# Statistics of a graph layer's later groups, four weight units and the first gathered tile at other places of a one-core kernel

## The chip, the cores and the metric

The kernel runs on one core of a Trainium2 chip. What counts is the device time of one execution in microseconds (us); three executions of the kernel before took 749.41 to 750.44 us, their median is 750.01 us.

## The reference

1250 nodes with 512 features, 40000 edges. A layer norm gives `xn`; a graph layer (own features and the mean over the neighbours, each through a 512x512 matrix, then a layer norm and a relu) and a linear attention over 8 heads are both taken from `xn` and added to `x`. Then follows a feed-forward part with a shared branch and eight experts, of which every node uses two:

```python
xn = _layernorm(x)
x = x + gnn(xn, edges) + mix(xn)
flat = _layernorm(x) * ln_scale + ln_bias
h_shared = swiglu(flat @ shared_in_w.T)              # 2 x 1024 columns
out_shared = h_shared @ shared_out_w.T + shared_out_b
...                                                  # group by argmax, two experts by top_k
h_expert = swiglu(flat @ expert_in_w.T)
for e in range(8):
    routed = routed + comb[:, e:e + 1] * (h_expert @ expert_out_weight[e].T)
return x + out_shared + routed
```

## The kernel before

The nodes lie in ten tiles of 125 rows, and the tiles in three groups, (0 to 3), (4 to 7) and (8, 9). Every matrix product is made of three fp16 products (`split3`, L1343): each operand is kept as a high half and a low half. The engines' programs are written out by hand, one after the other, and wait for each other by semaphores; there is no planner. What an engine does next is the order of its program alone.

**Weights** come in 30 units of 1 MB (`units`). SyncE loads unit u into one of two staging buffers when unit u-2 has been used up (L292). ScalarE then makes the high half (`unit`, L435) and VectorE the low half (`unit`, L745) and so tells that the unit is ready (`w_rdy`). Units 8 to 11 (`U_SIN`) are the shared input weights, 12 and 13 (`U_EXP`) those of expert 0, 14 and 15 those of expert 1, and so on; 28 and 29 are the shared output weights. Where a unit is made is a place in both programs.

**Graph layer and norms.** TensorE makes the ten products (`gnn`), ScalarE copies each out of its bank (L604), and VectorE takes group after group: `gnn_norm` (statistics L768 and L771, `rsqrt` L753 to L760 with a square root on ScalarE, L442, then L1115 and L1121), `ffn_norm` (L1128, statistics again, two `rsqrt`, L1139). TensorE then turns the four column blocks of the group (`yT`, L1614), ScalarE scales them (L612) and makes the high half (L615), VectorE the low half (`yT_low`, L1145). Between these stand the first products with the expert input weights (`hid_e`): two per tile on TensorE; ScalarE takes the silu (L623), VectorE multiplies (L1154), ScalarE copies (L627), GpSimd subtracts (L366) and writes the rows to `h_rows` in HBM (L369). A product of `hid_e` waits until the product two before it has been multiplied. In group 0 the statistics of `gnn_norm` also hold the making of units 4 to 7.

**Gate.** After tile 4 of `hid_e` VectorE works out the gate; the exponential is on ScalarE (L674).

**Shared products.** 24 products (`n` = 0 to 23, eight blocks of 128 columns for each group; 500 nodes wide for n below 16, 250 wide from 16 on), each 24 matmuls. For each: silu (L689), multiply (L1293), copy (L692), subtract on GpSimd (L390). A product waits until the one two before it has been multiplied (`h_f`). Units 12 to 15 are made in this stage. GpSimd writes the routing table in it, loads it back, and starts the first two gathers after its step 12.

**Experts.** The rows that each expert needs are gathered from `h_rows` in tiles of 128 (L377, 512 KB each, `gather(i)`), at most 28 tiles and a spare one (NG = 29), into two buffers. `gathered(i)` waits for the landing and raises `g_rdy` (L382). TensorE turns a tile (`turn`, 16 matmuls, L1701), ScalarE and VectorE copy it from the banks to `hgT` (L715/L705 and L1305/L1313), and 24 matmuls (`expert`, L1343) give the result. ScalarE copies that out (L710) and writes it to `y_rows` (L712); there is one buffer for it, so that copy waits for the write before. The number of tiles of each expert is read from a small table into registers (`borders`, L258). In this run 23 tiles are in use. GpSimd's order:

```python
            gathered(0)
            for i in range(1, NG):
                if i + 1 < NG:
                    pool.wait_ge(S["turned"], i)
                    gather(i + 1)
                gathered(i)
```

For the gathers that no expert uses, VectorE raises `turned` in TensorE's place (L1320) when `g_rdy` allows it, and ScalarE fills up the writes (L729). After the last gather GpSimd fetches the 20 blocks of results (L420, four buffers); VectorE adds them to `x` (L1327), then the shared output product of the tile (L1331), which TensorE has made by then (ten products, L1746 and L1343).

The attribution of a matmul in the profile is the line of its helper: L1343 is every `split3`.

Of the kernel before, what the change touches and what calls it, by code (L numbers as in the profile page):

```python
# [49 lines left out]
LATER = (4, 6)  # L50
NFIX = FIX * SUBS
# [39 lines left out]
def build(nc, a, out):  # L91
    with ExitStack() as ctx:
# [37 lines left out]
        hgT = xflat[:, 0:2 * ROWW].rearrange("p (z s j n) -> p z s j n", z=2, s=2, j=J)  # L130
        yb = xflat[:, 2 * ROWW:2 * ROWW + 2 * DIM].bitcast(F32)
# [121 lines left out]

        def borders(eng):

            ends = []
            for z in range(2):
                four = eng.value_load(etab[0:1, z:z + 1], min_val=0, max_val=PACK ** 4 - 1)  # L258
                for k in range(4):
                    e = 4 * z + k  # L260
                    ends.append(eng.snap((four // PACK ** k) % PACK + 1, min_val=e + 1, max_val=NT - EXP + e + 1))
            return ends
# [50 lines left out]
        def _(pool):  # L313
# [72 lines left out]
            for t0, nt in GROUPS:  # L386
                c0, w = t0 * P, nt * P
                for j in range(J):
# [10 lines left out]
                    if n == TILES + 2:  # L399
# [4 lines left out]
                        gather(1)  # L404
                    n += 1
            gathered(0)
            for i in range(1, NG):
                if i + 1 < NG:
                    pool.wait_ge(S["turned"], i)
                    gather(i + 1)  # L410
                gathered(i)
# [13 lines left out]
        def _(act):  # L425
# [246 lines left out]
            unit(U_SIN + 1)  # L672
            act.wait_ge(S["gt_req"], 1)
            s.activation(gt[:, 1], gt[:, 0], ACT.Exp).then_inc(S["gt_exp"], 1)  # L674
            for t in range(5, TILES):
                hid_e(t)
                if t in (5, 6):
                    unit(U_SIN + t - 3)
# [4 lines left out]
            for t0, nt in GROUPS:  # L683
                w = nt * P
                for j in range(J):
# [9 lines left out]
                    if n % 4 == 0 and n <= 16:  # L695
                        unit(U_EXP + n // 4 - 1)
                    if n == 21:
                        act.wait_ge(S["etab_rdy"], 1)
                        ends = borders(act)
                        total = ends[EXP - 1]  # L700

# [12 lines left out]
            act.wait_ge(S["turned"], 1)  # L714
            s.activation(hgT[:, 0, 0], turned[0], ACT.Copy).then_inc(S["hg_h"], 1)  # L715
# [17 lines left out]
        def _(dve):  # L733
# [376 lines left out]
            def gnn_norm(t0, nt, between=(), units=False):  # L1110
                ts = range(t0, t0 + nt)
                stats(xn, t0, nt, "gn_cp", units)
# [46 lines left out]
            gnn_norm(a0, n0, units=True)  # L1159
            ffn_norm(a0, n0)  # L1160
            yT_low(0)
# [3 lines left out]
            hid_e(0)  # L1165
            yT_low(4)
# [16 lines left out]
            unit(U_SIN + 1)  # L1183
# [27 lines left out]
            unit(U_SIN + 2)  # L1211
# [13 lines left out]
            unit(U_SIN + 3)  # L1225
# [52 lines left out]
            for t in range(7, TILES):  # L1278
                hid_e(t)
                if t == 8:  # L1280
                    route()
# [5 lines left out]
            for t0, nt in GROUPS:  # L1287
                w = nt * P
                for j in range(J):
# [7 lines left out]
                    if n % 4 == 0 and n <= 16:  # L1297
                        unit(U_EXP + n // 4 - 1)
# [500 lines left out]
```

## Time and profile before

| | us |
|---|---|
| median of three runs | 750.01 |
| profiled execution | 746.69 |
| its span (first to last instruction) | 744.7 |
| TensorE busy | 708.5 |
| VectorE busy | 386.4 |
| ScalarE busy | 261.9 |
| GpSimd busy | 174.4 |

Times of rows are us from the start of the span. In a row of the timeline stand start, duration, engine, line, operation, what is written and read, the number of instructions, and in brackets how long the engine stood idle before it and for whom. PE is TensorE, ACT is ScalarE, DVE is VectorE, POOL is GpSimd, SP is SyncE; PEclk is the granted clock as a share of 2.4 GHz.

### The profile page before, as it was taken

The numbers are of one execution on the slowest core, as the hardware profiler recorded it, in microseconds if no ns is written. First come the engines' busy times: TensorE is split into PE (matmuls) and PEld (weight loads), VectorE is DVE, ScalarE is ACT, GpSimd is POOL, SyncE is SP. The second block draws the span as 40 slices with busy tenths as digits, with TensorE's granted clock in tenths as the row PEclk, the third lists the DMA queues.
The fourth block names the chain that finished last, engine by engine and source line by source line (L and its number), as shares of the span: only waits on it lengthen the run. The fifth ranks groups of instructions, "written<-read, shape, count | busy, mean of one in ns | idle before, by whom it ended". The sixth has DMA issues, their size and how long they took to land.

```text
span 744.7 us, 12041 instructions
## 1 busy us (share of the span) xinstructions
PE 708.5 (95%) x4382; PEld 433.8 (58%) x4382; DVE 386.4 (52%) x735; ACT 261.9 (35%) x386; POOL 174.4 (23%) x170
## 2 busy tenths in 40 slices
PE   6989899997999999998999999999889999999998
PEld 5646577774576656565756644446745555555554
DVE  5874678964476757876246422222235523441154
ACT  4853123323652231356353123333336443532000
POOL 3340000000061000013222257742312212222362
PEclk9999999998999999999999999999999999999999
DMA  9200002000031150011325212222166766643675
GB/s 249 96 1 1 1 2 114 2 13 2 1 138 61 29 198 1 0 28 28 114 84 169 56 28 58 58 79 92 29 227 239 264 216 239 230 136 130 195 211 150
DMA packets 24417, 73.90 MB, mean 99 GB/s; under 512 B 7059, under 2 KB 7405, under 8 KB 20274
## 3 DMA queue, kind: packets, MB, share of 16 engines
q1 hardware_dynamic: 8607, 39.74, 15.8%
q0 software_dynamic: 10768, 25.52, 11.6%
q10 hardware_dynamic: 4994, 8.01, 2.9%
q8 instruction: 31, 0.51, 0.3%
q14 instruction: 17, 0.13, 0.1%
HBM read 57.90 MB, written 15.31 MB: 98 GB/s over the span
## 4 chain that ended last, share of the span: by engine, by line
PE 77%; DVE 11%; ACT 6%; issue 3%; DMA 3%; DVEq 0%; POOL 0%; SPq 0%; ACTq 0%; POOLq 0%
PE banks L1343 59%; PE banks L1392 6%; PE banks L1380 3%; PE banks L1701 3%; DMA y_rows<-xT 2%; DVE st L768 1%; PE banks L1572 1%; PE banks L1366 1%; ACT W L435 1%; DMA x<-in_x 1%; PE banks L1581 1%; DVE xn L1154 1%; DVE W L745 1%; PE banks L1373 1%; ACT big L612 1%
## 5 line engine op out<-in xcount | busy, mean ns | idle before, releaser
L1343 PE MATMUL banks<-W,xT 128*125 128x512 f16 (+1 forms) x1392 | 318.2, 383 | 8.0 <-ACT xT L710 2.2
L1343 PEld LDWEIGHTS banks<-W,xT 128*125 128x125 f16 (+2 forms) x1392 | 165.3, 122 | 137.4 <-issue 15.9
L1343 PE MATMUL banks<-xT,W 128*128 128x500 f16 (+1 forms) x720 | 131.0, 344 | 1.8 <-DVE xn L1293 1.4
L1343 PEld LDWEIGHTS banks<-xT,W 128*128 128x128 f16 x720 | 70.7, 99 | 60.5 <-issue 4.4
L745 DVE SCALAR_TENSOR_TENSOR W<-stg,W 128x2048 f16<-128x2048 f32 x30 | 68.5, 2304 | 40.9 <-ACT W L435 40.9
L1343 PE MATMUL banks<-W,big 128*125 128x512 f16 x360 | 81.5, 380 | 0.0
L1343 PEld LDWEIGHTS banks<-W,big 128*125 128x125 f16 x360 | 48.3, 136 | 29.2 <-issue 2.3
L377 POOL DMA_INDIRECT xn<-h_rows,tokidx x29 | 35.3, 1217 | 125.1 <-PE banks L1701 114.7
L366 POOL TENSOR_TENSOR big<-xn,big 125x512 f16<-125x512 f32 x20 | 23.5, 1173 | 174.7 <-ACT big L627 174.7
L1313 DVE CAST xT<-banks 128x1024 f32 x22 | 26.9, 1222 | 69.0 <-PE banks L1701 69.0
L435 ACT ACTIVATE W<-stg 128x2048 f16<-128x2048 f32 x30 | 56.4, 1903 | 0.0
L1392 PE MATMUL banks<-W,big 125*125 125x512 f16 x200 | 54.0, 393 | 0.6 <-ACT big L566 0.6
L360 POOL TENSOR_TENSOR x<-x,bproj 125x512 f32<-125x512 f32 x10 | 14.4, 1476 | 165.6 <-DVE big L1044 165.6
L1293 DVE SCALAR_TENSOR_TENSOR xn<-banks,xn 128x500 f32<-128x500 f32 (+1 forms) x24 | 14.2, 591 | 69.8 <-ACT xn L689 69.8
L710 ACT ACTIVATE xT<-banks 128x512 f32<-128x512 f32 x23 | 13.7, 597 | 66.9 <-PE banks L1343 41.5
L390 POOL TENSOR_TENSOR big<-xn,big 128x500 f16<-128x500 f32 (+1 forms) x24 | 22.7, 945 | 45.9 <-ACT big L692 45.9
L689 ACT ACTIVATE xn<-banks 128x500 f32<-128x500 f32 (+1 forms) x24 | 12.4, 516 | 52.8 <-PE banks L1343 47.5
L897 DVE TENSOR_TENSOR W<-big 125x2048 f16<-125x2048 f16 x23 | 28.1, 1223 | 3.3 <-DVE big L893 2.4
L1154 DVE SCALAR_TENSOR_TENSOR xn<-banks,xn 125x512 f32<-125x512 f32 x20 | 13.8, 690 | 30.5 <-ACT xn L623 30.5
L1701 PEld LDWEIGHTS banks<-ident,xn 128*128 (+1 forms) x384 | 24.0, 100 | 8.5 <-issue 1.8
L1701 PE MATMUL banks<-ident,xn 128*128 128x128 f16 x384 | 26.2, 223 | 2.9 <-POOLq L382 1.5
L420 POOL DMA_INDIRECT xT<-y_rows,sloti x20 | 24.7, 1236 | 16.1 <-issue 9.3
(324 smaller groups left out, 785.0 us busy)
## 6 DMA issues: line engine op xcount, KB each, us to landing
stg<-in_units SPq DMA_DIRECT2D x30, 1024.0 KB
y_rows<-xT ACTq DMA_DIRECT2D x29, 256.0 KB
h_rows<-big POOLq DMA_DIRECT2D x10, 500.0 KB, 3.6
out_x<-x SPq DMA_DIRECT2D x10, 224.0 KB
stg<-in_wqkT SPq DMA_DIRECT2D x2, 1024.0 KB, 11.0
x<-in_x SPq DMA_DIRECT2D x2, 896.0 KB
xn<-h_rows,tokidx POOLq DMA_INDIRECT x29, 5.3
x<-in_x SPq DMA_DIRECT2D x1, 448.0 KB
```

Source lines behind the costliest of these rows:

```text
L366: g.tensor_tensor(hrow[t % 2][:, HID + 512 * u:HID + 512 * (u + 1)], mscr[0:P, 1024 + 512 * u:1536 + 512 * u], hrow[t % 2][:, 512 * u:512 ...
L377: g.indirect_dma_start(hg[i % 2], None, h_rows, bass.IndirectOffsetOnAxis(ap=tokidx[:, i:i + 1], axis=0)).then_inc(g_in[i % 2], 16)
L390: g.tensor_tensor(hT[:, 1, j, c0:c0 + w], mscr[:, 1024 + 512 * (n % 2):1024 + 512 * (n % 2) + w], hT[:, 0, j, c0:c0 + w], ALU.subtract).th ...
L420: g.indirect_dma_start(yg[n % 4], None, y_rows, bass.IndirectOffsetOnAxis(ap=sloti[:, 0, k, t:t + 1], axis=0)).then_inc(yg_in[n % 4], 16)
L435: s.activation(W[:, u % NSLOT, 0, :], stg[:, u % NSTG, :], ACT.Copy, scale=WS).then_inc(S["w_h"], 1)
L745: v.scalar_tensor_tensor(out=W[:, u % NSLOT, 1, :], in0=stg[:, u % NSTG, :], scalar=WS, in1=W[:, u % NSLOT, 0, :], op0=ALU.mult, op1=ALU.s ...
L897: return v.tensor_tensor(ohw[g % RING], iotaP.unsqueeze(1).to_broadcast(every), kr[g % KRING].rearrange("p k (a b) -> p (k a) b", b=2).uns ...
L1313: v.tensor_copy(hgT[:, bass.ds((i + 1) % 2, 1), 1].rearrange("p z j n -> p (z j) n"), turned[1]).then_inc(S["hg_l"], 1)
L1343: ins = te.matmul(dst, lhs(sl, c), rhs(sr, c), start=(first and c == 0 and k == 0), stop=(last and c == n - 1 and k == 2))
L1380: ins = te.matmul(ps[q][:, o:o + WK], ohw[z][:, CH // 2 + k // 2, :, k % 2], ohw[z][:, k // 2, 0:WK, k % 2], start=(h == 0 and k == 0), st ...
L1392: ins = te.matmul(ps[4 + z][0:BLK, :], CT[z][0:P, t, :], xs[:, s, t, :], start=(t == 0 and s == 0), stop=(t == TILES - 1 and s == 1))
L1701: ins = te.matmul(turned[s][:, j, :], rows(s * HID + j * 128), ident16[:, :], start=True, stop=True)
```

## The change

1. `stats` of groups 1 and 2 is taken out of `gnn_norm` and stands ahead of it in VectorE's program: that of group 1 before `yT_low(0)`, that of group 2 before `yT_low(4)`.
2. Units 9, 10 and 11 are made after tiles 5, 6 and 7 of `hid_e`; before it was after tiles 4, 5 and 6. Units 12 to 15 are made after 4, 8, 11 and 14 shared products; before it was 4, 8, 12 and 16.
3. TensorE turns gathered tile 0 after shared product 22, ahead of product 23. Its copy goes to a buffer of its own (`hgT0`), and ScalarE and VectorE copy it between their steps for products 22 and 23. `expert(0)` reads that buffer and waits for the multiplication of product 22 instead of 23.
4. GpSimd raises `g_rdy` for tiles 0 and 1 after its steps 21 and 22. In the loop it waits for the landing of gather i+1 right after it has started it, where it waited for gather i.
5. TensorE reads the table of borders in two halves, after products 18 and 20; before it was after the first turn.

```diff
--- before.py
+++ after.py
@@ -48,6 +48,7 @@
 LATER = (4, 6)
+EXP_AT = [4, 8, 11, 14]
 NFIX = FIX * SUBS
...
 RING = 4
@@ -128,6 +129,7 @@
         hgT = xflat[:, 0:2 * ROWW].rearrange("p (z s j n) -> p z s j n", z=2, s=2, j=J)
+        hgT0 = mscr[:, 4096:5120].bitcast(F16).rearrange("p (s j n) -> p s j n", s=2, j=J)
         yb = xflat[:, 2 * ROWW:2 * ROWW + 2 * DIM].bitcast(F32)
@@ -251,15 +253,13 @@
+        def half_borders(eng, z):
...
+            four = eng.value_load(etab[0:1, z:z + 1], min_val=0, max_val=PACK ** 4 - 1)
+            return [eng.snap((four // PACK ** k) % PACK + 1, min_val=4 * z + k + 1, max_val=NT - EXP + 4 * z + k + 1) for k in range(4)]
...
         def borders(eng):
...
-            ends = []
-            for z in range(2):
-                four = eng.value_load(etab[0:1, z:z + 1], min_val=0, max_val=PACK ** 4 - 1)
-                for k in range(4):
-                    e = 4 * z + k
-                    ends.append(eng.snap((four // PACK ** k) % PACK + 1, min_val=e + 1, max_val=NT - EXP + e + 1))
-            return ends
+            return half_borders(eng, 0) + half_borders(eng, 1)
@@ -402,13 +402,13 @@
                         gather(1)
+                    if n in (3 * J - 3, 3 * J - 2):
+                        gathered(n - 3 * J + 3)
                     n += 1
-            gathered(0)
-            for i in range(1, NG):
-                if i + 1 < NG:
-                    pool.wait_ge(S["turned"], i)
-                    gather(i + 1)
-                gathered(i)
+            for i in range(1, NG - 1):
+                pool.wait_ge(S["turned"], i)
+                gather(i + 1)
+                gathered(i + 1)
             pool.nop().then_inc(S["g_rdy"], 1)
             pool.wait_ge(S["y_st"], 16 * (NT + 2))
@@ -669,13 +669,12 @@
             hid_e(4)
-            unit(U_SIN + 1)
             act.wait_ge(S["gt_req"], 1)
...
                 hid_e(t)
-                if t in (5, 6):
-                    unit(U_SIN + t - 3)
+                if t in (5, 6, 7):
+                    unit(U_SIN + t - 4)
             for z in range(2):
...
             n = 0
@@ -692,12 +691,15 @@
                     n += 1
-                    if n % 4 == 0 and n <= 16:
-                        unit(U_EXP + n // 4 - 1)
+                    if n in EXP_AT:
+                        unit(U_EXP + EXP_AT.index(n))
                     if n == 21:
...
                         total = ends[EXP - 1]
+                    if n == 3 * J - 1:
+                        act.wait_ge(S["turned"], 1)
+                        s.activation(hgT0[:, 0], turned[0], ACT.Copy).then_inc(S["hg_h"], 1)
             def high(i):
@@ -711,8 +713,6 @@
-            act.wait_ge(S["turned"], 1)
-            s.activation(hgT[:, 0, 0], turned[0], ACT.Copy).then_inc(S["hg_h"], 1)
             act.wait_ge(S["turned"], 2)
...
             unit(U_EXP + 4)
@@ -1107,9 +1107,8 @@
-            def gnn_norm(t0, nt, between=(), units=False):
+            def gnn_norm(t0, nt, between=()):
                 ts = range(t0, t0 + nt)
-                stats(xn, t0, nt, "gn_cp", units)
                 rsqrt(5, mv[:, t0:t0 + nt, 1], EPS * WS * WS, t0, nt)
...
                     ins = v.scalar_tensor_tensor(out=xn[:, t, :], in0=xn[:, t, :], scalar=mv[:, t, 0:1], in1=gam[:, :],
@@ -1156,13 +1155,16 @@
             late_constants()
-            gnn_norm(a0, n0, units=True)
+            stats(xn, a0, n0, "gn_cp", True)
+            gnn_norm(a0, n0)
             ffn_norm(a0, n0)
+            stats(xn, a1, n1, "gn_cp")
             yT_low(0)
...
             hid_e(0)
+            stats(xn, a2, n2, "gn_cp")
             yT_low(4)
...
             gnn_norm(a2, n2)
@@ -1180,7 +1182,6 @@
             hid_e(4)
-            unit(U_SIN + 1)
...
             logits = ps[5][0:P, 0:20 * TILES].rearrange("p (t s n) -> p t s n", t=TILES, s=2)
@@ -1208,7 +1209,7 @@
             hid_e(5)
-            unit(U_SIN + 2)
+            unit(U_SIN + 1)
             for k in range(EPG):
...
             v.memset(cnt9[:, :, 17:18], 1.0)
@@ -1222,7 +1223,7 @@
             hid_e(6)
-            unit(U_SIN + 3)
+            unit(U_SIN + 2)
             link(v.tensor_tensor(gt[:, 12, :, 0:1], gt[:, 8, :, 0:1], gt[:, 8, :, 1:2], ALU.add))
...
             link(v.reciprocal(gt[:, 12, :, 0:1], gt[:, 12, :, 0:1]))
@@ -1277,6 +1278,8 @@
                 hid_e(t)
+                if t == 7:
+                    unit(U_SIN + 3)
                 if t == 8:
...
             for z, (t0, nt) in enumerate(GROUPS):
@@ -1294,15 +1297,16 @@
                     n += 1
-                    if n % 4 == 0 and n <= 16:
-                        unit(U_EXP + n // 4 - 1)
+                    if n in EXP_AT:
+                        unit(U_EXP + EXP_AT.index(n))
                     if n == 21:
...
                         total = ends[EXP - 1]
...
-            dve.wait_ge(S["turned"], 1)
-            v.tensor_copy(hgT[:, 0, 1], turned[1]).then_inc(S["hg_l"], 1)
+                    if n == 3 * J - 1:
+                        dve.wait_ge(S["turned"], 1)
+                        v.tensor_copy(hgT0[:, 1], turned[1]).then_inc(S["hg_l"], 1)
...
             dve.wait_ge(S["turned"], 2)
...
             unit(U_EXP + 4)
@@ -1678,7 +1682,15 @@
                 ins.then_inc(S["cntT_mm"], 1)
+            def turn(rows):
+                for s in range(2):
+                    for j in range(J):
+                        ins = te.matmul(turned[s][:, j, :], rows(s * HID + j * 128), ident16[:, :], start=True, stop=True)
+                ins.then_inc(S["turned"], 1)
...
+            hg2 = mscr[:, 2048:4096].bitcast(F16)
             pe.wait_ge(S["w_rdy"], U_SIN + 4)
+            ends = []
             n = 0
...
                 w = nt * P
@@ -1692,34 +1704,28 @@
                     ins.then_inc(S["h_mm"], 1)
+                    if n in (18, 20):
+                        pe.wait_ge(S["etab_rdy"], 1)
+                        ends += half_borders(pe, (n - 18) // 2)
+                    if n == 3 * J - 2:
+                        pe.wait_ge(S["cntT_ev"], 3)
+                        pe.wait_ge(S["g_rdy"], 1)
+                        turn(lambda o: hg2[:, o:o + 128])
                     n += 1
...
-            def turn(rows):
-                for s in range(2):
-                    for j in range(J):
-                        ins = te.matmul(turned[s][:, j, :], rows(s * HID + j * 128), ident16[:, :], start=True, stop=True)
-                ins.then_inc(S["turned"], 1)
...
-            hg2 = mscr[:, 2048:4096].bitcast(F16)
             hgT2 = xflat[:, 0:2 * ROWW]
-            pe.wait_ge(S["cntT_ev"], 3)
-            pe.wait_ge(S["g_rdy"], 1)
-            turn(lambda o: hg2[:, o:o + 128])
-            pe.wait_ge(S["etab_rdy"], 1)
-            ends = borders(pe)
             total = ends[EXP - 1]
-            def expert(e, cur):
-                split3(ps[0][:, :], lambda s, c: hgT2[:, cur(s * HID + c * 128)], unitv(U_EXP + 2 * e), J, True, True).then_inc(S["me_mm"], 1)
+            def expert(e, lhs):
+                split3(ps[0][:, :], lhs, unitv(U_EXP + 2 * e), J, True, True).then_inc(S["me_mm"], 1)
...
             pe.wait_ge(S["w_rdy"], U_EXP + 2)
-            pe.wait_ge(S["h_f"], 3 * J)
-            expert(0, lambda o: slice(o, o + 128))
+            pe.wait_ge(S["h_f"], 3 * J - 1)
+            expert(0, lambda s, c: hgT0[:, s, c, :])
             for e in range(EXP):
...
                 with pe.Fori(1 if e == 0 else ends[e - 1], ends[e]) as i:
@@ -1730,7 +1736,7 @@
                     cur = pe.snap((i % 2) * ROWW)
-                    expert(e, lambda o: bass.ds(cur + o, 128))
+                    expert(e, lambda s, c: hgT2[:, bass.ds(cur + s * HID + c * 128, 128)])
...
             pe.wait_ge(S["h_rdy"], 3 * J)
```

## Rows read from the trace of the kernel before

**Rows 1.** The page's first part: busy time, share of the span and instructions.
```profile
PE 708.5 (95%) x4382; PEld 433.8 (58%) x4382; DVE 386.4 (52%) x735; ACT 261.9 (35%) x386; POOL 174.4 (23%) x170
```
**Rows 2.** Waits of PE in the whole span: us in total, times, longest us.
```profile
PE banks L1614 <- DVE xn L1139: 2.9, 2, 1.6
...
PE banks L1343 <- ACT xT L710: 2.2, 3, 1.8
...
PE banks L1343 <- DVE xn L1154: 2.0, 3, 0.9
```
**Rows 3.** Timeline of DVE around the norms of groups 1 and 2.
```profile
299.27 0.68 DVE L1145 TENSOR_TENSOR xT<-big,xT 128x500 f16<-128x500 f32 x1 [5.03 <-ACT xT L615]
...
301.18 2.47 DVE L768 BATCH_NORM_STATS2 st<-xn 125x6 f32<-125x512 f32 x4
303.68 0.38 DVE L771 BATCH_NORM_AGGREGATE mv<-st 125x2 f32<-125x6 f32 x4
...
308.32 1.27 DVE L1145 TENSOR_TENSOR xT<-big,xT 128x500 f16<-128x500 f32 x2
...
329.51 1.28 DVE L768 BATCH_NORM_STATS2 st<-xn 125x6 f32<-125x512 f32 x2
```
**Rows 4.** Timeline of ACT in the same stretch.
```profile
304.61 0.57 ACT L604 COPY xn<-banks 125x512 f32<-125x512 f32 x1
...
328.90 1.28 ACT L442 ACT_TABLE_LOAD   x1
```
**Rows 5.** Timeline of PE in the same stretch, two of its three waits.
```profile
336.19 10.57 PE L1343 MATMUL banks<-W,xT 128*125 128x512 f16 x48 [0.70 <-DVE xn L1154]
348.12 0.65 PE L1614 MATMUL banks<-ident,xn 125*128 125x125 f32 x4 [1.36 <-DVE xn L1139]
```
**Rows 6.** Timeline of ACT and PE around the gate.
```profile
376.67 1.90 ACT L435 ACTIVATE W<-stg 128x2048 f16<-128x2048 f32 x1
...
382.99 0.24 ACT L674 ACTIVATE gcat<-gcat 125x40 f32<-125x40 f32 x1 [3.12 <-DVE gcat L1205]
...
385.97 31.45 PE L1343 MATMUL banks<-W,xT 128*125 128x512 f16 x144 [0.86 <-DVE xn L1154]
```
**Rows 7.** Timeline of ACT and PE where the shared products become narrow.
```profile
512.81 1.89 ACT L435 ACTIVATE W<-stg 128x2048 f16<-128x2048 f32 x1
...
517.41 15.54 PE L1343 MATMUL banks<-xT,W 128*128 128x250 f16 x144 [1.38 <-DVE xn L1293]
```
**Rows 8.** Timeline of PE after shared product 23, and one stretch of the windows.
```profile
534.46 1.05 PE L1701 MATMUL banks<-ident,xn 128*128 128x128 f16 x16 [1.51 <-POOLq L382]
536.88 1.86 PE L1701 MATMUL banks<-ident,xn 128*128 128x128 f16 x16 [1.36 <-DVE xT L1305]
...
553.53 2.76 PE L1343 MATMUL banks<-W,xT 128*128 128x512 f16 x12 [1.85 <-ACT xT L710]
...
536.00:538.80 2.80, 1.92 (x17) 1.84 (x18) 0.80 (x2) 0.59 (x2) 0.75 (x1) 0.58 0.47 118
```
**Rows 9.** GpSimd's step 23; landings of all gathers, of that at 566.31; border loads; first result's write.
```profile
534.34 0.62 POOL L390 TENSOR_TENSOR big<-xn,big 128x250 f16<-128x250 f32 x1 [1.90 <-ACT big L692]
...
DMA to landing us min/median/max: 4.1/5.3/9.2
...
DMA to landing us min/median/max: 9.0/9.0/9.0
...
L258 PEldq TENSOR_LOAD <-etab x2: 306/316/326, 534.5 to 535.2; - x2
...
545.45 7.28 DMA y_rows<-xT
```
**Rows 10.** Timeline of POOL and DVE behind the experts.
```profile
685.03 0.94 POOL L377 DMA_INDIRECT xn<-h_rows,tokidx  x1 [4.81 <-DVE rs L1320]
...
698.85 1.22 POOL L420 DMA_INDIRECT xT<-y_rows,sloti  x1 [5.91 <-issue]
...
741.28 0.69 DVE L1331 SCALAR_TENSOR_TENSOR x<-banks,x 125x512 f32<-125x512 f32 x1 [2.00 <-PE banks L1343]
```


## Prediction before the run

> **What bounds the kernel now.** I read the page's busy times first: PE is busy for 708.5 of 744.7 us [rows 1], so whatever shortens the run must close one of PE's waits, and work moved on another engine counts only through such a wait. The list of PE's waits [rows 2] shows which lie in the reach of the change: 2.9 us in two waits for the norm (the longer 1.6, the other 1.36), 2.0 in three waits for the multiplications of L1154, 2.2 mainly in one wait for the first result's copy. The timeline then says what each wait hangs on [rows 3 to 8], and the landings of the gathers and the stretch behind the experts show what the new order of GpSimd must live with [rows 9, 10].
>
> **Statistics sooner.** VectorE stands idle for 5.03 us ahead of its first low half of group 0, until 299.27, then runs the statistics of group 1 in 2.47 + 0.38 us, from 301.18 to 304.06 [rows 3]. The four tiles are copied by then (the last at about 297.9), so all of it fits into the idle time and 2.9 us leave the chain. Not all arrive: the low halves of column blocks 2 and 3 (308.32, [rows 3]) wait for ScalarE, whose next step is the copy at 304.61 [rows 4]. That one sat behind a square root which now comes earlier, but TensorE's product for it ends only at about 303.7; so these halves come some 1.7 us sooner. PE's 1.56 us wait before the turns of group 1 then goes. The same for group 2: its statistics (1.28 us at 329.51 [rows 3], and the aggregation, together 1.5) go into VectorE's wait of 2.0 us for ScalarE, and the table load that follows at 328.90 on ScalarE [rows 4] moves with the chain. That gives 1.7 + 1.3 = 3.0 us on VectorE. PE's remaining waits there are 0.70 and 1.36 [rows 5]; with the 1.56 they sum to 3.6, of which the chain gives back 3.0, and about 0.6 of the last stays. **-3.0 us**. Bounds: 1.7 (only group 1's part arrives) and 3.6.
>
> **Units 9 to 11 later.** Today ScalarE makes the high half of unit 9 at 376.67 for 1.90 us, ahead of the gate's exponential, for which it then waits until 382.99; PE waits 0.86 us at 385.97 for the multiplication behind it [rows 6]. Without the unit here the gate's chain ends some 4 us sooner, more than the wait. **-0.9 us**. The three units meet the same load one tile later; the last is made after tile 7, while VectorE idles about 4.5 us per product there. Their transfers on SyncE's queue start when the unit two before is made, so they also shift; the last must be there some 25 us later and nothing in that stretch waits for a transfer. If that cover were gone, PE would wait at product 0 for unit 11. Bounds: 0 and 0.9.
>
> **Units 14 and 15 at 11 and 14.** Unit 15 is made at 512.81, as the products turn from 5.1 to 2.6 us each, and PE waits 1.38 us for it [rows 7]. After product 13 there are 5.1 us per product, of which the unit takes VectorE 2.3 and ScalarE 1.9. **-1.4 us**; bounds 1.0 and 1.4. The loads of units 16 and 17 follow their predecessors sooner and end before they are needed.
>
> **First tile turned ahead.** Removed: the wait of 1.51 before the first turn, that of 1.36 before the second, and the slow clock that followed them: granted 0.58 between 536.0 and 538.8, where 16 turns took 1.86 instead of 1.05 and the matmuls behind them some 0.6 more [rows 8]. So 1.51 + 1.36 + 0.8 + 0.6 = 4.3 us. The copies of tile 0 (1.0 and 1.2 us) lie beside product 23 (2.6 us). The border loads of TensorE's sequencer take 0.3 us a piece, 0.7 a half with the register work [rows 9]; PE has more matmuls than that queued ahead, since the loads of 534.5 ran under the turns of 534.46. I cost them at 0; if the queue were empty, 1.4.
>
> Added: a wait that GpSimd's order brings. Call the end of product 23 zero. Step 23 of GpSimd starts 1.4 later (534.34 against 532.95), takes 0.62 [rows 9], and gather 2 stands behind it in the queue: it starts at 2.2, though its buffer is free since before product 23. Landing takes at least 4.1 [rows 9]; 4.6 gives 6.8. TensorE, now without waits, has turned tile 1 and finished expert tile 0 at 6.3 and wants tile 2: a wait of 0.6. Gather 3 now also waits for that landing and starts at 7.15, in the midst of the loads of units 18 and 19, which begin at about 6.6 and 8.8. Gathers in that position land in 8.3 to 9.2 us (six of the 22 in the loop; the row of 9.0 is one), the others in 4.1 to 5.7 [rows 9]. So tile 3 is there at about 15.9, and TensorE wants it at 13.2: a wait of 2.8. Today's wait of 1.85 at 553.53 [rows 8], for the first result's write (7.28 us [rows 9]), falls into the same time and is covered by it. Sum: -4.3 - 1.85 + 0.6 + 2.8 = **-2.8 us** (to a tenth, which the positions give too: expert tile 2 starts 20.6 after zero today, 16.85 + 0.9 then). Bounds: -4.5 (gather 3 lands in time for the write's copy) and -1.1 (the wait of 2.8 brings the clock down once more, some 1.7).
>
> **In the loop** only one gather is under way at a time. It is started 0.3 us after its buffer is free and wanted 11.6 after, so a landing of 9 alone is hidden; one after a late one has less. Started again at each landing, GpSimd needs landing + 0.45 per tile, TensorE 6.26. With 5.3 GpSimd gains 0.5 per tile. **0 us**; bounds 0 and the rival below.
>
> **Behind the experts** 23 tiles are used, so gathers 26, 27 and 28 serve nothing but hold the queue: they start at 685.03, 686.27 and 692.01, two under way, and the result fetches start at 698.85 [rows 10]. From now on each waits for the one before. Gather 26 with ScalarE's writes beside it 5.5 (6.2 today, shared with 27), then 4.4 and 4.3 alone, 0.3 between: the fetches start 2.1 later (0.7 to 4.6). They last about 40 us, held by four buffers and the landings, and end 2.00 before TensorE's last product [rows 10]. So the chain passes to them: 2.1 - 2.0, and I add for landings under load: **+0.5 us**, bounds 0 and 2.6. The Trainium skill (DMA: Bandwidth & Descriptors, Anatomy of one DMA) speaks against serial transfers in general: about 2.0 us of each transfer is fixed, mostly the wait for the receipt, and the rest is bytes over 436 GB/s. For 512 KB that is an estimate of 3.2 us, with which the three gathers would end no later than today and this term would be 0; the shortest landing here is 4.1, and I keep the rows.
>
> **Sum**: -3.0 - 0.9 - 1.4 - 2.8 + 0.5 = -7.6 us, from 746.7 to 739.1 for the profiled execution. The median of the runs stands 3.3 above that execution; I carry the same difference over: 750.0 - 7.6 = **742.4 us**. A measurement of this kernel can tell about 0.2% (1.5 us) from no change.
>
> **Rivals.**
> *Both ends of GpSimd's new order cost more* (0.19). Gather 3 takes 9.2, the clock falls in the wait (+1.7), the fetches start 4.6 late (+2.1 over my term). For it: six landings near 9, two of today's last gathers took 6.2 and 7.6. Against: those two overlapped. -7.6 + 3.8 = -3.8: 746.2 us.
> *The statistics don't arrive at TensorE* (0.08). If group 2's square roots stay where they are because ScalarE's table loads end the chain, only 1.7 of 3.0 come, and if the gate's 0.9 stays with it: -7.6 + 1.3 + 0.9 = -5.4, 744.6 us. Against: ScalarE waited for VectorE before each of these roots.
> *The change gives what it saves to another wait* (0.05): a transfer that doesn't depend on TensorE's time. Then 750 us. Against: PE's list shows no wait for a transfer, only one for a write.
> *The loop becomes bound by gathers* (0.05), the slower side. Its place is the wait for landing in GpSimd's loop. Six landings of 9 and sixteen of about 4.8 make a mean of 5.9, and with 0.45 that is 6.4 against TensorE's 6.26: nearly equal. In the early experts, where two units load for every two tiles, it is already 6.8. If it were 6.8 throughout, each of 20 tiles would cost 6.8 + 0.45 - 6.26 = 1.0: 742.4 + 20 = 762 us; it eats the whole gain from a mean of 6.2 on. Against it: the long landings overlap the next gather and the unit loads, and a delayed gather meets less of both. The Trainium skill (SBUF — State Buffer, SBUF: two separate sides) says that a GpSimd DMA's descriptors wait while VectorE holds the shared port pair, which would lengthen serial gathers further; the trace agrees in kind: such an issue takes 0.94 us, and 2.2 beside VectorE's unit steps.
>
> **How the numbers follow.** My case has 0.63, with 740.2 to 745.5 as its own range (all upper bounds of gain; or the clock and half of the tail). To it come 746.2 and 744.6, and 1.1 for spread: 740.2 to 747.3 holds about 0.87. Faster by over 0.2%: 0.63 + 0.19 + 0.08 = 0.90. Within: 0.05. Slower: 0.05.
>
> **What would show it.** Right: no PE wait at L1614 above 0.8 us; none of 0.86 near tile 5 of `hid_e` and of 1.38 at the first narrow products; product 23 behind the first turn without a gap; PE waits of about 0.6 and 2.8 at the turns of tiles 2 and 3 for L382; fetches that start about 16.7 after the last expert tile; VectorE's last step no longer waiting for PE. Wrong: PE waits for L382 again and again in the loop, or clock below 1.00 there.

## The result, and the profile after

The changed kernel takes 753.68 us (median of 8 runs, 752.05 to 759.17) against 749.71 us for the kernel before in the same series (746.58 to 752.06): a ratio of 1.0083, 95% interval 1.0057 to 1.011. By the ratio it is slower by about 6 us (the medians lie 4.0 us apart), where I had forecast 7.6 less. Its profiled execution took 753.01 us, with a span of 751.1 us (before: 744.7).

First the busy times on the page of the changed kernel, to hold against [rows 1]:

```profile
PE 716.9 (95%) x4382; PEld 437.4 (58%) x4382; DVE 387.7 (52%) x735; ACT 262.3 (35%) x386; POOL 174.7 (23%) x170
```

The same 4382 matmuls keep PE busy 8.4 us longer, so it isn't waits alone; some of them ran more slowly. The waits of PE in the changed kernel (us in total, times, longest), beside [rows 2]:

```profile
PE banks L1688 <- POOLq L382: 5.3, 4, 2.3
...
PE banks L1364 <- DVE xn L777: 1.6, 1, 1.6
PE banks L1347 <- ACT xT L712: 1.3, 2, 1.1
PE banks L1618 <- DVE xn L1138: 0.9, 1, 0.9
```

The waits that the first two parts were to close are gone or short: 0.9 is left of 2.9 for the norms. (The 1.6 for L777 stands at 12.7 us, ahead of all that was changed; it is 0.65 in the kernel before.) New in the expert loop is a wait for L382, GpSimd's message that a gathered tile has landed, four times; the kernel before has one such wait, ahead of the loop [rows 8]. And in the list of all engines' waits GpSimd itself now stands still for landings:

```profile
POOL xn L377 <- DMA xn<-h_rows,tokidx: 99.0, 18, 8.0
```

Yet its gathers don't land later on the whole: their median is 4.4 us, where it was 5.3 [rows 9].

```profile
DMA to landing us min/median/max: 4.2/4.4/9.4
```

**Up to the experts** the change did what it was to do. The timeline of PE in the changed kernel at four landmarks (start, duration, ..., idle before and for whom):

```profile
313.28 10.54 PE L1347 MATMUL banks<-W,xT 128*125 128x512 f16 x48 [0.72 <-issue]
347.19 0.65 PE L1618 MATMUL banks<-ident,xn 125*128 125x125 f32 x4 [0.94 <-DVE xn L1138]
...
427.52 4.80 PE L1347 MATMUL banks<-xT,W 128*128 128x500 f16 x22 [0.44 <-DVE xn L1153]
...
526.51 1.06 PE L1688 MATMUL banks<-ident,xn 128*128 128x128 f16 x16
```

The first stands at 311.08 in the kernel before, so the changed kernel's profiled execution came to it 2.2 us late; the code up to there is the same (see the last section). The second is 348.12 there [rows 5]: from 2.2 behind to 0.9 ahead, 3.1 us won by the statistics. The third stood at 429.69: 2.2 ahead, 1.2 won at the gate. At the fourth product 22 ends, at 526.67 (the turn's first matmul starts 0.2 before that). In the kernel before it ended at 530.4 (by [rows 8]: 534.46 less the wait of 1.51 and product 23's 2.6). So the changed kernel is 3.7 ahead, 1.5 of it won by unit 15.

**In the expert loop** all this is lost. (In what follows tiles and gathers are counted from 0.) PE's timeline, the first turns and those around the third wait:

```profile
526.51 1.06 PE L1688 MATMUL banks<-ident,xn 128*128 128x128 f16 x16
527.40 2.72 PE L1347 MATMUL banks<-xT,W 128*128 128x250 f16 x24
529.96 1.06 PE L1688 MATMUL banks<-ident,xn 128*128 128x128 f16 x16
530.85 5.34 PE L1347 MATMUL banks<-W,xn 128*128 128x512 f16 x24
536.93 2.17 PE L1688 MATMUL banks<-ident,xn 128*128 128x128 f16 x16 [0.74 <-POOLq L382]
539.09 5.35 PE L1347 MATMUL banks<-W,xT 128*128 128x512 f16 x24
546.77 2.16 PE L1688 MATMUL banks<-ident,xn 128*128 128x128 f16 x16 [2.32 <-POOLq L382]
548.87 7.04 PE L1347 MATMUL banks<-W,xT 128*128 128x512 f16 x24
...
583.09 2.21 PE L1688 MATMUL banks<-ident,xn 128*128 128x128 f16 x16 [2.00 <-POOLq L382]
585.18 6.10 PE L1347 MATMUL banks<-W,xT 128*128 128x512 f16 x24
591.12 1.06 PE L1688 MATMUL banks<-ident,xn 128*128 128x128 f16 x16
592.19 5.35 PE L1347 MATMUL banks<-W,xT 128*128 128x512 f16 x24
597.38 2.16 PE L1688 MATMUL banks<-ident,xn 128*128 128x128 f16 x16
```

Tile 0 is turned, product 23 follows without a gap, tile 1 is turned: as planned. Then the waits of 0.74 and 2.32 at tiles 2 and 3 that the prediction had worked out (0.6 and 2.8). But there is a third of 2.00 at tile 8 and a fourth of 0.26 at tile 20, and a turn behind a wait takes 2.2 us instead of 1.06; so does that at 597.38 (tile 10), where the list shows no wait. GpSimd's timeline says why tile 8 is late:

```profile
563.33 2.23 POOL L377 DMA_INDIRECT xn<-h_rows,tokidx  x1 [4.70 <-PE banks L1688]
573.52 2.49 POOL L377 DMA_INDIRECT xn<-h_rows,tokidx  x1 [7.97 <-DMA xn<-h_rows,tokidx]
583.62 0.94 POOL L377 DMA_INDIRECT xn<-h_rows,tokidx  x1 [7.60 <-DMA xn<-h_rows,tokidx]
```

SyncE's timeline has the loads of units, two stretches of it:

```profile
562.57 2.53 SPq L292 DMA_DIRECT2D stg<-in_units  x2
...
575.24 2.53 SPq L292 DMA_DIRECT2D stg<-in_units  x2
```

Gather 7 starts at 563.33 in the loads of two units and lands 9.4 us later. Gather 8 may only start then, at 573.52, 4.2 us after its buffer was free (the turn of tile 6 ends at 569.3). The next two units begin to load 1.7 us later, and it takes 9.3 us too. PE wanted tile 8 at 581.1, 11.8 us after that buffer was free; 4.2 and 9.3 make 13.5, and with GpSimd's message the tile is 2.0 late. Gather 9 starts at 583.62. In the kernel before, gathers 7 to 10 started at fixed steps of 6.26 us, the pairs of loads at 565.55, 578.07 and 590.61, and only every second gather met a pair: 9.0, 5.1, 9.2, 5.4.

**Behind the experts** the fetches of results start 18.4 us after the first output product (14.55 before, [rows 10]; forecast 16.7), and VectorE's last step no longer waits for PE. First output product, first fetch and last step of the changed kernel:

```profile
688.88 0.42 PE L1752 MATMUL banks<-etabs 18*125 18x512 f16 x1
...
707.28 1.22 POOL L420 DMA_INDIRECT xT<-y_rows,sloti  x1 [4.43 <-issue]
...
747.68 0.69 DVE L1335 SCALAR_TENSOR_TENSOR x<-banks,x 125x512 f32<-125x512 f32 x1
```

From output product to last step: 58.8 us, 57.0 before (741.28 less 684.30). The account of the spans is then: 2.2 from the late start, -3.1, -1.2, -1.5 up to product 22, +8.3 from the end of product 22 to the output products (162.2 us against 153.9), +1.8 behind them. That makes 6.5; the spans differ by 6.4.

### The profile page after: what moved, and what is told of

The parts are those of the page before. It is cut to its first block, busy times and chain, and to the rows that moved or that the text cites. A ratio compares the mean times of both kernels' runs of the same rounds, so it can differ in the third digit from the quotient of the medians.

```text
span 751.1 us, 12043 instructions
## 1 busy us (share of the span) xinstructions
PE 716.9 (95%) x4382; PEld 437.4 (58%) x4382; DVE 387.7 (52%) x735; ACT 262.3 (35%) x386; POOL 174.7 (23%) x170
## 4 chain that ended last, share of the span: by engine, by line
PE 68%; DMA 14%; DVE 8%; ACT 5%; issue 3%; POOL 1%; DVEq 0%; POOLq 0%; SPq 0%; ACTq 0%
PE banks L1347 50%; DMA xn<-h_rows,tokidx 9%; PE banks L1396 6%; DMA xT<-y_rows,sloti 4%; PE banks L1384 3%; PE banks L1688 2%; PE banks L1576 1%; DMA y_rows<-xT 1%; PE banks L1370 1%; DMA x<-in_x 1%; DVE st L768 1%; PE banks L1585 1%; ACT xn L588 1%; ACT xn L585 1%; ACT big L612 1%
## 5 line engine op out<-in xcount | busy, mean ns | idle before, releaser
L1347 PEld LDWEIGHTS banks<-W,xT 128*125 128x125 f16 (+1 forms) x1368 | 164.3, 123 | 133.9 <-issue 18.8
L1347 PEld LDWEIGHTS banks<-xT,W 128*128 128x128 f16 x720 | 70.7, 98 | 58.8 <-issue 4.3
L1688 PE MATMUL banks<-ident,xn 128*128 128x128 f16 x384 | 30.9, 223 | 5.3 <-POOLq L382 5.3
L1688 PEld LDWEIGHTS banks<-ident,xn 128*128 (+1 forms) x384 | 26.3, 98 | 14.0 <-issue 7.6
L1347 PE MATMUL banks<-W,xn 128*125 128x512 f16 (+1 forms) x144 | 32.8, 379 | 0.0
L707 ACT ACTIVATE xT<-banks 128x1024 f32 x22 | 22.5, 1024 | 23.5 <-PE banks L1688 22.7
## 6 DMA issues: line engine op xcount, KB each, us to landing
stg<-in_wqkT SPq DMA_DIRECT2D x2, 1024.0 KB, 11.4
```

Source lines behind the costliest of these rows:

```text
L707: s.activation(hgT[:, bass.ds(i % 2, 1), 0].rearrange("p z j n -> p (z j) n"), turned[0], ACT.Copy).then_inc(S["hg_h"], 1)
L1347: ins = te.matmul(dst, lhs(sl, c), rhs(sr, c), start=(first and c == 0 and k == 0), stop=(last and c == n - 1 and k == 2))
L1688: ins = te.matmul(turned[s][:, j, :], rows(s * HID + j * 128), ident16[:, :], start=True, stop=True)
```

## Experiments

Two theories at first. **S**: the loss comes from GpSimd's new order, each landing waited for right behind its own start. **E**: it comes from the early start of the experts, whose loads, writes and gathers then collide, whatever GpSimd's order.

### The changed kernel with the old order of GpSimd's loop (e1)

```diff
-            for i in range(1, NG - 1):
-                pool.wait_ge(S["turned"], i)
-                gather(i + 1)
-                gathered(i + 1)
+            for i in range(1, NG):
+                if i + 1 < NG:
+                    pool.wait_ge(S["turned"], i)
+                    gather(i + 1)
+                if i > 1:
+                    gathered(i)
```

> The changed kernel with GpSimd's old order in the gather loop: gather i+1 is started first, then the landing of gather i is waited for; all else of the change stays. Theory S (the landing waited for right behind its own start costs the time, in the loop and behind the experts): 9 us less than the kernel before, so about 740, ratio 0.988: 3.1, 1.2 and 1.5 from the norms and the units, 3.7 from the early turn; no wait of PE for L382 but 0.6 at tile 2, fetches 14.6 us after the last expert tile. Theory E (the early start of the experts is what hurts, by collisions of loads, writes and gathers whatever GpSimd's order): 750 or more.

Measured: 736.58 us, the kernel before 747.42 in the same series, ratio 0.9873 (0.9831 to 0.9915). Two kinds of waits are left to PE in the loop:

```profile
PE banks L1349 <- ACT xT L714: 1.5, 5, 0.6
...
PE banks L1690 <- POOLq L382: 0.7, 1, 0.7
```

So the early start of the experts does no harm, and four lines of order turn 0.8% lost into 1.3% won. E is out as the main cause. The landings are as long as in the kernel before, longer in the median than those of the changed kernel:

```profile
DMA to landing us min/median/max: 4.1/5.4/9.3
```

### The kernel before with the new order alone (e2)

```diff
             gathered(0)
-            for i in range(1, NG):
-                if i + 1 < NG:
-                    pool.wait_ge(S["turned"], i)
-                    gather(i + 1)
-                gathered(i)
+            gathered(1)
+            for i in range(1, NG - 1):
+                pool.wait_ge(S["turned"], i)
+                gather(i + 1)
+                gathered(i + 1)
```

> The kernel before, with only the landing of gather i+1 waited for right behind its start. Theory S: 4 to 7 us slower than before (about 754 to 757): 2 behind the experts, the rest in waits of PE for L382 with slow clock behind them. Theory E: only the 2 us behind the experts (752).

Measured: 758.68 us, ratio 1.0172 (1.0126 to 1.0218), 11 us slower, more than either theory had expected. The experts start late here and it still costs, so S holds, but my price was too low. PE's waits for L382 (1.51 of the 7.4 stand ahead of the loop, as in the kernel before), and the three turns behind the others:

```profile
PE banks L1701 <- POOLq L382: 7.4, 4, 3.6
```

```profile
549.48 2.16 PE L1701 MATMUL banks<-ident,xn 128*128 128x128 f16 x16 [1.59 <-POOLq L382]
...
587.35 2.27 PE L1701 MATMUL banks<-ident,xn 128*128 128x128 f16 x16 [3.58 <-POOLq L382]
...
602.40 2.16 PE L1701 MATMUL banks<-ident,xn 128*128 128x128 f16 x16 [0.73 <-POOLq L382]
```

### Parts 1 and 2 of the change alone (e3)

The kernel before with the edits of parts 1 and 2 of the change, as the diff shows them.

> The kernel before with parts 1 and 2 of the change only (statistics sooner; units 9 to 11, 14 and 15 at other steps). Theory S and E: 5.9 us less (3.1 + 1.25 + 1.55, the positions of the changed kernel's trace), about 743.8, ratio 0.992. Should these gains be lost again downstream (third theory, U): 749 to 750.

Measured: 739.19 us, ratio 0.9900 (0.9868 to 0.9932), 7 to 8 us less, somewhat more than the 5.9 expected. These gains reach the end; nothing downstream takes them back (U is out).

### The early turn alone, old order of GpSimd (e4)

The kernel before with parts 3 and 5 of the change, the earlier `g_rdy` of part 4 and the loop of e1.

> The kernel before with the first tile turned ahead of product 23 and the borders read in halves, but GpSimd's loop in its old order and none of parts 1 and 2. Theory S: 3.7 us less than before (746). Theory E: 752 or more, since the experts start early here too.

Measured: 744.76 us, ratio 0.9973 (0.9945 to 1.0000): 2.7 us less, by the interval nearly no difference. Not slower, as E wanted, and less than S said. Why is seen from stretches of the traces. From the end of product 22 to the first output product it takes 153.9 us in the kernel before, 150.6 here (the first turn starts at 535.26, the output product at 686.06), 150.5 in e1. But in e3, which has no early turn, it is 151.1: its two waits of 1.5 and 1.4 are there, yet no slow clock follows them and PE doesn't wait for the first result's write, where it waited 1.85 in the kernel before. So 3 us of the 153.9 are a slow passage that is not in every execution. The early turn by itself is worth about 0.5 us over a run without that passage, since gather 2, held back behind GpSimd's step 23, makes PE wait in its place.

The passage isn't peculiar to one execution of the kernel before either. Of the six profiles in which tile 0 is turned behind product 23, those of the kernel before and of the statistics alone (the last group of experiments) have it, and four don't (e2, e3 and the two other single parts). The second turn, first with the statistics alone, then in e2:

```profile
535.70 1.87 PE L1703 MATMUL banks<-ident,xn 128*128 128x128 f16 x16 [1.36 <-DVE xT L1307]
...
535.40 1.05 PE L1701 MATMUL banks<-ident,xn 128*128 128x128 f16 x16 [1.36 <-DVE xT L1305]
```

None of the eight profiles with the early turn has it at that place. The 81 times of the kernel before fall in two groups, 17 from 741.57 to 743.94 us and 64 from 746.23 on; the gap is about as wide as the passage is long. That the slower group is the one with the passage is a guess, since only one of its executions was profiled.

### The new order only in the loop (e8), only behind the experts (e9)

Against e1:

```diff
                 if i + 1 < NG:
                     pool.wait_ge(S["turned"], i)
                     gather(i + 1)
-                if i > 1:
-                    gathered(i)
+                if i < 24:
+                    gathered(i + 1)
+                elif i > 24:
+                    gathered(i)
```

> The changed kernel, where GpSimd waits for each landing right behind its start only up to gather 24 (the tiles that the 23 in use need) and goes back to the old order for the gathers behind the experts. If the loss lies in the expert loop (theory L): within 2 us of the changed kernel, 11 to 12 us over the run with the old order (e1), ratio to before about 1.005. If it lies behind the experts (theory B): like the run with the old order, ratio about 0.988.

Measured: 751.34 us, ratio 1.0050 (1.0025 to 1.0076). In e9 it is the other way round (`gathered(i)` up to 24, then `gathered(i + 1)` as well):

> The other way round: the old order up to gather 24, the new order for gathers 26 to 28. Theory L: 1.9 us over the run with the old order (e1), as the two traces differ behind the experts, ratio 0.990. Theory B: 11 to 13 us over it.

Measured: 740.17 us, ratio 0.9911 (0.9880 to 0.9943). So the loop costs 1.8% over e1, the gathers behind the experts 0.4%: 13 and 3 us, and the changed kernel's 2.1% over e1 is about their sum. The 0.4% alone are no more than the intervals are wide; the traces show the 3 us. From the second turn to the first output product they have 147.2 us (e1), 146.6 (e9), 159.5 (e8) and 158.9 (the changed kernel), and from the output product to VectorE's last step 57.0 (e1) and 60.0 (e9).

### Small unit loads (e7, e7b)

Both kernels leave out nearly all bytes of the loads of units 18 to 29. Making the units stays.

```diff
-                sp.dma_start(stg[:, u % NSTG, :], a["units"][u]).then_inc(stg_in[u % NSTG], 16)
+                c = 2048 if u < 18 else 16
+                sp.dma_start(stg[:, u % NSTG, 0:c], a["units"][u][:, 0:c]).then_inc(stg_in[u % NSTG], 16)
```

> The changed kernel, with only 16 of 2048 columns of units 18 to 29 loaded (those experts' weights are then mostly stale); all waits stay. Theory C (the long landings beside unit loads make the new order late): no landing above 6 us in the loop and no wait of PE for L382 behind tile 2; at most 3 us over the next run. Theory O (GpSimd's wait and restart cost the time by themselves): 10 us or more over it.

> The same small loads with GpSimd's old order. Theory C: ends like the run before it, but for the 2 us behind the experts, and 0 to 2 us below the run with the old order and full loads (e1). Theory O: 10 us or more below the run before it.

Measured: 738.82 us with the new order (ratio 0.9892, 0.9865 to 0.9920) and 736.91 with the old (0.9871, 0.9825 to 0.9917). The 13 us of the loop are gone: 145.65 us from the second turn to the output products with the new order, 145.88 with the old. In e7 one wait for GpSimd's message is left (L383 there), that of tile 2, and the landings are short:

```profile
PE banks L1689 <- POOLq L383: 0.6, 1, 0.6
```

```profile
DMA to landing us min/median/max: 4.1/4.5/5.7
```

Theory C holds: in the loop GpSimd's order is harmless by itself and costs only where a gather meets a pair of unit loads. The same run answers what the prediction's slower rival said of VectorE and the shared port: GpSimd's instruction beside VectorE's unit steps takes 2.2 us in e7 too (gathers 9, 11, 15 and 19), and these gathers land in 5.6 to 5.7 us. That is about 1.3 us more than the others, a small part of the 9; the rest goes with the loads.

### Gather 2 ahead of step 23 (e6)

```diff
                     if n in (3 * J - 3, 3 * J - 2):
                         gathered(n - 3 * J + 3)
+                    if n == 3 * J - 2:
+                        pool.wait_ge(S["turned"], 1)
+                        gather(2)
```

(on top of e1, with the loop's first gather left out)

> The run with the old order (e1), and gather 2 started before GpSimd's step 23 instead of behind it. In e1 PE waits 0.7 us for tile 2 and the turn behind that wait takes 2.19 us instead of 1.06. Theory S: both go, 1.8 us under e1, ratio to before 0.985. Rival: gather 2 is no longer last there, but the first result's write is (PE waited 0.57 for it in e1), and less than 1 us comes: ratio 0.987.

Measured: 734.92 us, ratio 0.9859 (0.9819 to 0.9898), the fastest kernel of this study; 1.7 us under e1 by the medians, within the spread of both. The trace shows it more sharply. PE, from the first turn on:

```profile
524.38 1.06 PE L1694 MATMUL banks<-ident,xn 128*128 128x128 f16 x16
525.27 2.72 PE L1353 MATMUL banks<-xT,W 128*128 128x250 f16 x24
527.84 1.06 PE L1694 MATMUL banks<-ident,xn 128*128 128x128 f16 x16
528.73 5.34 PE L1353 MATMUL banks<-W,xn 128*128 128x512 f16 x24
533.91 1.16 PE L1694 MATMUL banks<-ident,xn 128*128 128x128 f16 x16
535.01 5.35 PE L1353 MATMUL banks<-W,xT 128*128 128x512 f16 x24
```

Neither the wait nor the slow turn is left, and so far the result's write makes no wait; it takes 147.8 us from the first turn to the output products (from 524.38 to 672.18), where e1 has 150.7: 2.9 us. The 1.8 expected were 0.7 and 1.1; most of the rest are waits for the write, 1.5 us in five places of e1 and one of 0.2 here. Here the early turn gets its worth.

### Each early part alone

The kernel before with one part each: the statistics, units 9 to 11, units 14 and 15.

> The kernel before with the statistics of groups 1 and 2 sooner, nothing else. By the term of the prediction 3.0 us less (ratio 0.996); by the trace of the changed kernel 3.1. Rival: 1.7 or less.

> The kernel before with units 9 to 11 one tile later, nothing else. Term of the prediction: 0.9 us less (ratio 0.9988); the changed kernel's trace gives 1.2 there. Too small for the interval of the times, so the positions of its trace decide: PE's wait of 0.86 us near tile 5 gone, and no other in its place.

> The kernel before with units 14 and 15 made after 11 and 14 shared products, nothing else. Term of the prediction: 1.4 us less (ratio 0.998), PE's wait of 1.38 us at the first narrow products gone.

Measured, in this order: 744.02 us, ratio 0.9953 (0.9923 to 0.9982); 742.89 us, 0.9970 (0.9940 to 0.9999); 742.68 us, 0.9941 (0.9917 to 0.9965). By the ratios these are 3.5, 2.2 and 4.4 us. The times are coarser than the terms, and the third is more than its term of 1.4 beyond its interval (2.6 to 6.2 us). Its profile lacks the slow passage of 3 us that the one of the kernel before has; whether that is the part's doing is open. In the traces each removes its own waits and no other; with the statistics alone these are one of 1.56, 0.4 of that of 1.36, and that of 0.70, which the term had counted in. What is left of the waits of [rows 2], with the statistics alone, with the gate's units alone, and with unit 15 sooner:

```profile
PE banks L1616 <- DVE xn L1138: 0.9, 1, 0.9
```

```profile
PE banks L1343 <- DVE xn L1153: 1.1, 2, 0.7
```

```profile
PE banks L1344 <- DVE xn L1155: 2.0, 3, 0.9
```

In the third the wait of 1.38 us of [rows 7] no longer appears.

## Why the prediction was wrong

The profile was forecast at 7.6 us less and its span is 6.4 longer, 14.0 us apart. Of these the three early parts have 1.7 (the late start of 2.2, less 0.5 that they won over their terms), the first tile 3.5, the loop from expert tile 2 on 7.5 and the end 1.3. Point by point, by the prediction's own steps:

**Statistics sooner, -3.0:** right; 3.1 in the trace, with 0.94 left of PE's last wait (I said 0.6). VectorE's statistics of the fourth tile wait for ScalarE's copy and still end before the low half they were put ahead of could start.

**Units 9 to 11, -0.9:** 1.2. I had counted only the wait of 0.86. **Units 14 and 15, -1.4:** 1.5.

**First tile turned ahead, -2.8:** the two new waits were right, they came at their places and nearly in their sizes (0.74 and 2.32 for 0.6 and 2.8). The sum was not. From the end of product 22 to the start of expert tile 2 it takes 22.2 us, in the kernel before 23.2: 1.0 won, not 2.8. The turns behind both waits cost 1.1 us more each, which I had not in the sum. Then the clock fell in the wait at tile 3, as my bound had it (7.04 us for 5.35 of matmuls, 1.7 more), and 0.7 are lost, outside the bounds of 4.5 and 1.1 won. Two of the terms taken as gains, the slow clock behind the removed waits (1.4) and the wait of 1.85 for the write, come together and not in every execution (see e4): behind the second turn's 1.87 us the run with the statistics alone waits 1.68 for the write, and without it PE waits there between nothing and 0.7.

**In the loop, 0:** this is the step that failed. I took the overlap there for granted: I wrote that a landing of 9 alone is hidden, and that "a delayed gather meets less of both". The first half is right: behind the landings of 9.1 at 619.68 and 9.4 at 644.77 no PE wait followed at once. The second half is wrong. In the early experts two units load for every two tiles. With two gathers under way, GpSimd started them by PE's turns, and every second one met a pair of loads. With one under way, a long landing pushes the next start out of step by 4 us, into the next pair. The long ones then follow each other (9.4, 9.3; in e2 8.9, 11.3; in e8 9.1, 10.3), and the second is late by its own length and by that delay. e7 shows that it is these loads and e8 that it is the loop.

The slower rival named this place. I gave it 0.05 and argued it away with a mean. Its condition, a mean of 6.2 us or more over the loop, did not even come true: gathers 3 to 24 of the changed kernel land in 5.8 us in the mean, and in 5.9 in the kernel before. A mean was the wrong measure. With two buffers GpSimd can't get further ahead than they allow, so the short landings later on don't pay for two long ones in a row (gathers 7 to 10 have a mean of 7.9). Its price was off as well: not 1.0 us for each tile, but four slow turns more than e1 has, three of them behind waits. The loop's 11.7 us over e1 (158.9 against 147.2) come out as 4.6 of waits for L382 (5.3 less 0.7), four more slow turns of 1.1, and about 2.4 of slow clock behind two waits (7.04 and 6.10 us for 5.35): 11.4.

**Behind the experts, +0.5:** 1.8 by the changed kernel's trace, 3 us by e9; inside the bound of 2.6 or just above it. Gathers 26 to 28 landed in 5.4, 5.4 and 4.3 us, near what I took (5.5, 4.4, 4.3), but between a landing and the next start lay 0.8 us, not 0.3: VectorE's message (L1324) stands in between. The estimate of 3.2 us for 512 KB that I worked out from the Trainium skill (DMA: Bandwidth & Descriptors, Anatomy of one DMA) would have put this term at 0; no gather here landed in under 4.0 us, so the rows were the better guide. How a landing splits into a fixed part and one that grows with the bytes, as that section has it, no run here shows.

**The range:** the terms' own bounds on the side of gain add up to 10.4 us with nothing lost behind the experts, which is 739.6 and not the 740.2 that I took. Nothing hangs on it: the miss lies on the other side.

## What to carry to other kernels

A wait for a landing right behind its own start makes the start of the next transfer depend on the last landing. That was free here while landings were even (e7); where another queue's loads come in bursts, one late transfer slips into the next burst. Neither a landing time measured with two under way nor a mean shows it: lay the starts and the bursts side by side. Keep the wait one step behind the start, and look at which instruction stands before the first start in its queue: in this kernel those two edits to GpSimd's program turned 0.8% slower into 1.4% faster.

Read a wait's price from what follows it too: here the turn behind a wait cost 1.1 us more, as much again as the shorter waits themselves, and behind two of the longer ones the clock fell.

## What the runs showed of the hardware

**A loop with addresses from registers has a slow pace that showed only behind a wait or an empty queue.** The turn at 583.09 and that at 591.12 of the changed kernel are the same 16 matmuls. Queries of their line in both stretches (durations ns min/median/max):

```profile
L1688 PEldq FUSED_REGOPS  x16: 46/46/110, 582.9 to 584.9; - x16
L1688 PE MATMUL banks<-ident,xn x16: 227/286/287, 583.1 to 585.0; 128*128 128x128 f16 x16
...
L1688 PE MATMUL banks<-ident,xn x16: 219/219/219, 591.1 to 592.0; 128*128 128x128 f16 x16
```

Each matmul of the turn has a register instruction of PE's sequencer before it. In the fast turn they don't appear: by then they have run, under the long matmuls of the expert before. After the sequencer has itself waited for a semaphore, matmuls and register instructions keep step: 16 matmuls in 2.2 us, 0.13 apart. It is not the clock: the turn at 583.09 had a granted clock of 0.57, but that at 546.77 had 1.00 and took 2.16, and in e1 the turn behind the wait takes as long in a stretch with the full clock (columns: stretch, length, PE, PEld, DVE, ACT, POOL busy, PEclk, DMA share, GB/s):

```profile
533.30:535.60 2.30, 2.23 (x17) 1.59 (x18) 1.85 (x1) 0.10 (x1) 0.00 (x0) 1.00 0.89 223
```

At 597.38 no idle time is shown at all, and the turn is still slow: its tile's gather had landed just in time (589.50 and 7.6 make 597.1). Nor is it the wait alone. The first two turns stand ahead of the loop and have fixed addresses and no register instructions, and behind waits of 1.51 and 1.36 us they take 1.05 at the full clock (e2, whose second turn is shown above). That the register instructions set the pace is read from this; no loop without them was run.

**The same code runs at two clocks in the same early stretch.** From 85 to 92 us the granted clock was 0.51 in the changed kernel's profiled execution, nearly all of it at the lower level of 1.2 GHz, and 0.76 in that of before, about half of it at 2.4 GHz, with the same program and the same waits up to there but for the one at 12.7 us:

```profile
85.00:92.00 7.00, 7.00 (x16) 2.83 (x14) 3.63 (x11) 0.24 (x1) 0.00 (x0) 0.51 0.00 1
```

```profile
85.00:92.00 7.00, 7.00 (x45) 3.83 (x43) 5.26 (x13) 0.60 (x1) 0.00 (x0) 0.76 0.00 1
```

This is 1.6 of the 2.2 us by which one came late to the norms; 0.5 had come at 12.7 us. Such spells came and went in other runs at about 44, 187 and 214 us too (granted 0.72 from 42 to 48 in e3, 1.00 in e1; 0.79 from 210 to 218 in e6, 1.00 in e1), and after product 23. Over this study 80 of 81 runs of the kernel before took 741.57 to 752.06 us, so parts of 1 to 3 us have to be read from landmarks in the trace, not from the times.
